# Transposing the softmax maxima of both attentions in bf16 parts, with their copy on ScalarE in both

## The chip, the cores and the metric

The kernel runs as one launch on 1 core of one Trainium2 chip. The metric is the device time of that core in microseconds (us), lower is better. The engines are named as in the profile: PE is TensorE (PEld its weight loads), DVE is VectorE, ACT is ScalarE, POOL is GpSimd, SP is the queue that issues most DMAs.

## What is computed

The input x has 128 sequences of 64 tokens with 128 features, and the context ctx has the same shape. Four blocks follow, each added to x:

```
x = x + attention0(layernorm(x), ctx, ctx, mask)      # 16 heads of 8 features
x = x + ffn0(layernorm(x))                            # 32 experts, top 4
x = x + attention1(layernorm(x), ctx, ctx)            # 16 heads, rotary positions
x = x + ffn1(layernorm(x))                            # 8 experts, top 2

attention:  score = (q @ k.T) / sqrt(8)               # per sequence and head, 64 x 64
            p     = softmax(score, axis=-1)           # subtracts the row's maximum
            out   = (p @ v) @ Wo + bo
```

The change touches the two attentions alone: the way in which each query's maximum reaches the transposed scores from which the exponentials are taken.

## The kernel before, in words

The 8192 tokens are 64 tiles of 128 rows. An attention handles two tiles (four sequences) in one iteration and has 32 iterations; the loop is software-pipelined by hand. Each engine has a `body(i, on)` that works on several iterations at once: `i.at(1)` is the next one, `i.at(-1)` the one before, `i.at(-3)` the third before, and so on. The first four and the last ones are written out; in between a hardware loop holds two iterations. The four blocks of the network follow one another, with the sorting of tokens to experts between them, and experts run after each attention. `attention(layer)` builds both attentions; `layer` 0 takes `body` on DVE and PE, layer 1 `body_with_sums` (DVE) and `body_with_rotation` (PE).

Scores are made twice. `scores(i)` writes the scores of four groups of heads (`UNITS`, r = 0 to 3) with queries on partitions into four PSUM banks `U_[r]`. DVE reduces each bank to its row maxima: `score_unit` (L579), four reductions of 128x512 to 128x8. `turned(i)` then writes the same scores into the same banks with keys on partitions, in which form the exponentials can be multiplied with the values at once. The maximum now belongs to a column, so it has to be subtracted by a matmul:

- `maxima(i)` (L864) turns the maxima `mx` by two fp32 transposes into bank `R_`. It waits for `score_max`, which the fourth reduction raises to its last value.
- In layer 0, `max_rows` on DVE (L586) copies the 128x256 result to `mxT`. In layer 1, ACT does this copy (L810). Either raises `mx_here`.
- `turned(i)` issues the mask matmuls (L873, bf16, layer 0 only), 32 fp32 matmuls of keys by queries (L878), waits for `mx_here`, and issues 16 fp32 matmuls (L890) that subtract the maxima: a constant `max_to` with -1 in the row of the wanted head, times `mxT`. The last four of them raise `t_psum`, on which ACT's exponentials (`exps`, L708) wait.

The order on each engine is the order in which `body` calls its parts. It is written out by hand, and an engine waits at the head of its own list:

- PE, layer 0: scores(i), inputs(next), values(previous), projections(next), rows_turned(i-3) (L972), maxima(i), turned(i), gate(i-3) (L984), output(previous) (L959, L963), next_values(next) (L946). In layer 1 the rotated projections follow turned(i) (L935 and L936 again, by their shared helper), and inputs comes last.
- DVE, layer 0: input statistics (L534, L539), four reductions (L579), the copy (L586), the reciprocal and the division (L619, L621), the gate's logits (L596), the top-k, the output's addition (L643) and its statistics. In layer 1 also the rotary weighting (L627) and the sums of the expert results (L557 to L562).
- ACT, layer 0: the inputs' copy (L788), values (L736), expert rows (L755), the doubled context (L795), the copy of turned rows (L801), keys and queries (L726, L728), `add_normalised` (L768), and then the exponentials (L708), `normalise` (L778).
- POOL, layer 0: among small operations two spreads of keys and queries (L442). Layer 1: eight indirect gathers of expert results per iteration (L419) among small operations.

`hold(engine, semaphore, value)` is a wait followed by an empty instruction, so that the wait is over before the next instruction starts. PE's outputs to `R_` in `maxima` and `output` use the same columns, one after the other.

Of the kernel before, what the change touches and what calls it, by code (L numbers as in the profile page):

```python
# [17 lines left out]
BF16 = mybir.dt.bfloat16  # L18
# [8 lines left out]
P = 128  # L27
# [75 lines left out]
def build(nc, a, out, ts, ys, yt, bias_parts):  # L103

    with ExitStack() as ctx:
        def sb(name, shape, dt=F32):
            return ctx.enter_context(nc.sbuf_tensor(name, shape, dt))
# [37 lines left out]
        sel_of = sb("sel_of", [P, 512], BF16)  # L145
        mx = sb("mx", [P, 2 * P])
        bo3 = [sb(f"bo3_{q}", [P, D], BF16) for q in range(2)]
# [37 lines left out]
        def setup():  # L185
# [39 lines left out]
            def fill(dve):  # L225

                nc.vector.memset(mask_u8.bitcast(F32), 0.0).then_inc(mask_zero, 1)
                nc.vector.memset(power[:], -0.5)
                nc.vector.memset(ones_b[:], 1.0)
                nc.vector.memset(ones_f[:], 1.0)  # L230
                nc.vector.memset(mx[:], 0.0)

            def convert(dve):
# [3 lines left out]
                nc.vector.tensor_copy(seq_of[:], seq_f)  # L237
                nc.vector.tensor_copy(sel_of[:], sel_f)
                nc.vector.tensor_scalar(gate_w[:, 0:E0], gate_w[:, 0:E0], bias_t[:, 8:9], None, ALU.mult)
                dve.wait_ge(mask_in, 16 * 2 * UNITS)  # L240
# [46 lines left out]
            def clear_values(pool):  # L287

                for q in range(2):
# [17 lines left out]
                 "mx_here", "t_psum", "probs", "o_psum", "o_recip", "o_normed", "wo_psum",  # L307
                 "added", "stats_r", "moments_r", "pool_r", "rstd_r", "mean_r", "neg_r", "neg_a", "rows_added", "t_ready", "tt_psum", "tt",
                 "gate_psum", "logits", "top8", "chosen", "top_kept", "row_sum", "combined", "mask_here", "mean_a")
        s = {n: sem(n) for n in names}  # L310

        def attention(layer):
# [10 lines left out]
            Mk = None if layer else carve2(2 * S, BF16)  # L323
            mxT = carve(2 * P)
            Pt = [carve(512) for _ in range(UNITS)]
# [41 lines left out]
            with nc.Block() as block:  # L367
# [162 lines left out]
                def _(dve):  # L530
# [44 lines left out]
                    def score_unit(i, r):  # L575

                        g4 = i.g * UNITS
                        dve.wait_ge(s["score_psum"], g4 + r + 1)
                        nc.vector.tensor_reduce(mx[:].rearrange("p (w c) -> p w c", w=2)[:, :, 32 * r:32 * r + 4],  # L579
                                                U_[r][:, :].rearrange("p (w j k) -> p w j k", w=2, j=4), AX.X, ALU.max  # L580
                                                ).then_inc(s["score_max"], 1)

                    def max_rows(i):

                        dve.wait_ge(s["mx_psum"], i.g + 1)
                        nc.vector.tensor_copy(mxT, R_[:, 0:2 * P]).then_inc(s["mx_here"], 1)  # L586

# [63 lines left out]
                    def body(i, on):  # L651
                        ex, pv, p3 = i.at(2), i.at(-1), i.at(-3)
                        if on(2):
                            hold(dve, x_in[ex.par], (ex.half + 1) * 16)
                            stats(ex, small["st_a"], small["mv_a"], "stats_a", "moments_a")
                        if on(0):
                            for r in range(UNITS):
                                score_unit(i, r)
                            max_rows(i)
                        if on(-1):  # L660
                            divide(pv)
                        if on(-3):
                            read_logits(p3)
                        if on(2):
                            offsets(ex)
                        if on(-3):
                            choose(p3)
                        if on(-1):
                            add_output(pv)
                            output_stats(pv)  # L670

                    def body_with_sums(i, on):
                        nx, pv, p3 = i.at(1), i.at(-1), i.at(-3)
                        if on(0):
                            for r in range(UNITS):
                                score_unit(i, r)
                        if on(-1):
                            divide(pv)
# [26 lines left out]
                def _(act):  # L705
# [78 lines left out]
                    def body(i, on):  # L784
# [21 lines left out]
                        if on(2) and layer:  # L806
                            normalise(ex)
                        if on(0) and layer:
                            act.wait_ge(s["mx_psum"], i.g + 1)
                            nc.scalar.activation(mxT, R_[:, 0:2 * P], ACT.Copy).then_inc(s["mx_here"], 1)  # L810
# [13 lines left out]
                def _(pe):  # L824
# [35 lines left out]
                    def maxima(i):  # L860

                        pe.wait_ge(s["score_max"], (i.g + 1) * UNITS)
                        for w in range(2):
                            last = nc.tensor.transpose(R_[:, w * P:(w + 1) * P], mx[:, w * P:(w + 1) * P], ident[:])  # L864
                        last.then_inc(s["mx_psum"], 1)

                    def turned(i):
# [18 lines left out]
                        for j in range(2):  # L886
                            for r, u in tiles_rb:
# [3 lines left out]
                                    U_[r][64 * u:64 * u + 64, :].rearrange("p (t j q) -> p t j q", t=4, j=2)[:, :, j, :],  # L891
                                    max_to[rows, at:at + S], mxT[rows, :].rearrange("p (t q) -> p t q", t=4),
                                    start=False, stop=True, skip_group_check=True)
# [1070 lines left out]
```

## Time and profile before

| what | value |
|---|---|
| median of 3 runs | 1782.54 us (1778.4 to 1782.55) |
| profiled execution, span | 2270.0 us, mean granted PE clock 0.830 |
| PE busy | 1668.9 us (74%) |
| DVE busy | 1187.1 us (52%) |
| ACT busy | 941.9 us (41%) |
| POOL busy | 1124.3 us (50%) |

The profiled execution is 487 us longer than the median of the runs without a profile; its span is the only time of its own that is shown. In its 40 slices the first attention takes the first 345 us, the second one the stretch from about 1025 to 1666 us; the rest is the sorting and the experts. A line of the profile gives start, length, engine, line, operation and shapes; what stands in square brackets is how long the engine had been idle before it, and what ended that.

### The profile page before, as it was taken

The page shows a single profiled execution, that of the slowest core. Times are in us where ns is not written, and L with a number is a line of the kernel's source. Part 1 is how long each engine was busy: PE and PEld are TensorE (multiplying, and loading weights), DVE is VectorE, ACT ScalarE, POOL GpSimd, SP SyncE. Part 2 cuts the span into 40 slices and gives each one's busy share as a digit, 9 for nine tenths or more (in the row PEclk, how much of TensorE's full clock was granted, in tenths as well). Part 3 has the DMA queues.
Part 4 walks back from the last instruction along what each step waited for, and adds up shares of the span by engine and source line. Part 5 has one row for each costly group of instructions (what it writes and reads, how often), then busy time and mean ns, then how long its engine had stood idle before and what let it go on. Part 6 is the DMA issues. An engine that isn't in the chain of part 4 may idle for free. (4 is left out here: it accounts for less than half of the span.)

```text
span 2270.0 us, 58116 instructions
## 1 busy us (share of the span) xinstructions
PE 1668.9 (74%) x20814; PEld 1246.6 (55%) x20815; DVE 1187.1 (52%) x3485; ACT 941.9 (41%) x2258; POOL 1124.3 (50%) x1456
## 2 busy tenths in 40 slices
PE   6999993947877777826777767777855777777876
PEld 4777771437766677713444444444533555556654
DVE  5778777935555555623455455455666111222245
ACT  3777772723333333413334334344535233333322
POOL 4777761055555565464454454454212555555553
PEclk9999996967787777756888788778875898999888
DMA  4111110012323232521211111111000111111154
GB/s 169 44 42 36 41 30 13 1 44 77 82 77 79 77 85 78 75 59 63 84 41 37 34 40 36 34 39 37 24 14 15 37 40 37 41 40 40 39 143 140
DMA packets 136997, 122.89 MB, mean 54 GB/s; under 512 B 27675, under 2 KB 121915, under 8 KB 136123
## 3 DMA queue, kind: packets, MB, share of 16 engines
q0 software_dynamic: 26624, 56.35, 10.5%
q1 hardware_dynamic: 110078, 64.47, 9.3%
q8 instruction: 68, 1.11, 0.2%
q10 hardware_dynamic: 192, 0.67, 0.1%
q14 instruction: 35, 0.29, 0.0%
HBM read 80.24 MB, written 41.18 MB: 53 GB/s over the span
## 5 line engine op out<-in xcount | busy, mean ns | idle before, releaser
L1488 POOL DMA_INDIRECT arena<-expert_rows,token_of_slot x432 | 413.4, 957 | 402.0 <-issue 221.1
L419 POOL DMA_INDIRECT arena<-slot_results,slot x256 | 246.7, 964 | 118.5 <-issue 86.8
L1879 DVE TENSOR_TENSOR arena<-bank,arena 128x352 f32<-128x352 f32 x144 | 75.5, 524 | 354.3 <-ACT arena L1858 245.4
L1723 POOL DMA_INDIRECT token_results<-arena,slot x144 | 141.1, 980 | 189.9 <-DVE arena L1887 157.0
L909 PE MATMUL bank<-arena,Vp 128*32 128x64 f32 x4096 | 142.8, 230 | 114.6 <-issue 113.1
L1826 PE MATMUL bank<-W,arena 128*128 (+1 forms) x864 | 141.1, 305 | 108.9 <-ACT arena L1865 54.8
L1586 PE MATMUL bank<-arena 128*128 128x128 f32 x1152 | 195.7, 338 | 30.3 <-ACT arena L1633 12.7
L1826 PEld LDWEIGHTS bank<-W,arena 128*128 128x128 f32 (+1 forms) x864 | 127.2, 213 | 164.2 <-issue 156.7
L1812 PE MATMUL bank<-W,arena 128*128 x576 | 214.8, 500 | 1.7 <-ACT arena L1870 1.7
L1586 PEld LDWEIGHTS bank<-arena 128*128 128x128 f32 x1152 | 183.9, 249 | 39.7 <-issue 39.6
L619 DVE RECIPROCAL arena<-bank 128x256 f32<-128x256 f32 x64 | 112.1, 1752 | 173.6 <-PE bank L915 173.6
L909 PEld LDWEIGHTS bank<-arena,Vp 128*32 128x32 f32 x4096 | 90.5, 112 | 168.2 <-issue 166.8
L432 POOL TENSOR_TENSOR arena<-arena,power 128x2 f32<-128x2 f32 x64 | 57.6, 899 | 243.8 <-DVE arena L547 241.0
L579 DVE TENSOR_REDUCE mx<-bank 128x8 f32<-128x512 f32 x256 | 158.3, 680 | 26.7 <-PE bank L853 24.0
L1614 PE MATMUL bank<-W,arena 128*128 x576 | 142.0, 362 | 35.8 <-issue 35.5
L708 ACT ACTIVATE arena<-bank 128x512 f32<-128x512 f32 x256 | 132.2, 603 | 70.4 <-PE bank L890 70.4
L442 POOL TENSOR_TENSOR arena<-arena,fixed 128x1024 f32<-128x1024 f32 x64 | 121.3, 1917 | 50.5 <-ACT arena L726 50.5
L801 ACT ACTIVATE arena<-bank 128x256 f32<-128x256 f32 x64 | 24.5, 383 | 286.0 <-PE bank L972 286.0
L1614 PEld LDWEIGHTS bank<-W,arena 128*128 128x128 f32 x576 | 112.2, 238 | 54.2 <-issue 45.3
L1864 ACT ACTIVATE arena<-bank 128x256 f32<-128x256 f32 x144 | 55.2, 383 | 204.6 <-remote 111.1
L1812 PEld LDWEIGHTS bank<-W,arena 128*128 128x128 f32 x576 | 108.5, 210 | 39.1 <-issue 12.6
L1681 DVE TENSOR_SCALAR arena<-bank,arena 128x128 f32<-128x128 f32 x288 | 99.2, 344 | 51.3 <-remote 34.4
(215 smaller groups left out, 3622.8 us busy)
## 6 DMA issues: line engine op xcount, KB each, us to landing
slot_results<-arena SPq DMA_DIRECT2D x72, 256.0 KB
arena<-in_ctx SPq DMA_DIRECT2D x64, 128.0 KB
expert_rows<-arena SPq DMA_DIRECT2D x64, 128.0 KB
arena<-token_results SPq DMA_DIRECT2D x32, 256.0 KB
arena<-expert_rows,token_of_slot POOLq DMA_INDIRECT x432
W<-in_w SPq DMA_DIRECT2D x4, 1032.0 KB
X<-in_x SPq DMA_DIRECT2D x32, 128.0 KB, 2.1
arena<-slot_results,slot POOLq DMA_INDIRECT x256
```

The lines of the kernel that those rows point to most:

```text
L419: nc.gpsimd.indirect_dma_start(out=gb[i.par][:, to:to + D], out_offset=None, in_=ys, in_offset=bass.IndirectOffsetOnAxis(ap=slot[:, at, k: ...
L442: nc.gpsimd.tensor_tensor(dst[i.par].rearrange("p (b j k) -> p b j k", b=4, j=4), src[i.par].rearrange("p (b k) -> p b k", b=4).unsqueeze( ...
L579: nc.vector.tensor_reduce(mx[:].rearrange("p (w c) -> p w c", w=2)[:, :, 32 * r:32 * r + 4], U_[r][:, :].rearrange("p (w j k) -> p w j k", ...
L619: nc.vector.reciprocal(rec, O_[:, 2 * D:4 * D]).then_inc(s["o_recip"], 1)
L708: nc.scalar.activation(Pt[r], U_[r][:, :], ACT.Exp, scale=SCALE).then_inc(s["probs"], 1)
L909: nc.tensor.matmul(O_[32 * r:32 * r + 32, 64 * sq:64 * sq + 64], Vp[i.par][:, at:at + 32], Pt[r][:, 128 * sq + 64 * j:128 * sq + 64 * j + 64],
L1488: nc.gpsimd.indirect_dma_start(out=XE[n % R][:, c * ROW:(c + 1) * ROW], out_offset=None, in_=ts, in_offset=bass.IndirectOffsetOnAxis(ap=to ...
L1586: last = nc.tensor.matmul(H_[2 * i.par + half][:, at:at + P], Wc[i.par][:, c * W1_0 + u * F0:c * W1_0 + (u + 1) * F0], XT[i.par][:, c * P: ...
L1614: last = nc.tensor.matmul(y, HA[pv.par][:, c * P:(c + 1) * P], W0b[:, bass.ds(x_e, 1), :], start=False, stop=True, skip_group_check=True)
L1723: nc.gpsimd.indirect_dma_start(out=yt[half], out_offset=bass.IndirectOffsetOnAxis(ap=row_of_slot[:, at:at + 1], axis=0), in_=YE[n % 4][:, ...
L1812: last = nc.tensor.matmul(H_[2 * r + u][:, 0:F1], XT[i.par][:, c * P:(c + 1) * P], W1a[:, bass.ds(x_e, 1), u * F1:(u + 1) * F1], start=Tru ...
L1826: last = nc.tensor.matmul(Y_[j.par][:, d * P:(d + 1) * P], AT[d % 2][0:f, k * P:(k + 1) * P], W1b[0:f, bass.ds(x_e, 1), k * P:(k + 1) * P] ...
```

## The change

The maxima are split on DVE into three bf16 parts that add up to the fp32 value (`split_maxima`: a cast, a subtraction, a cast, a subtraction, each waiting for the one before). `mx` becomes compact (128x32), and the parts lie in `mx_parts`, three groups of four columns in each 32. `maxima` turns them by two bf16 matmuls with a bf16 identity, and waits for the fourth step of the split in place of the fourth reduction. `mxT` is bf16, and the constant `max_to` is bf16 with -1 in three rows per head, so the 16 matmuls of `turned` are bf16 and sum the parts. DVE's copy in layer 0 (`max_rows`) goes; ACT makes the copy in both layers, after `add_normalised` and before the exponentials.

```diff
-        mx = sb("mx", [P, 2 * P])
+        mx = sb("mx", [P, 2 * UNITS * 4])
+        mx_parts = sb("mx_parts", [P, 2 * P], BF16)
+        ident_b = sb("ident_b", [P, P], BF16)
+        max_to_b = sb("max_to_b", [P, 4 * S], BF16)
...
                 nc.vector.tensor_copy(sel_of[:], sel_f)
+                nc.vector.tensor_copy(ident_b[:], ident)
+                nc.vector.tensor_copy(max_to_b[:], max_to)
...
-            mxT = carve(2 * P)
+            mxT = carve(2 * P, BF16)
...
-                    def max_rows(i):
-
-                        dve.wait_ge(s["mx_psum"], i.g + 1)
-                        nc.vector.tensor_copy(mxT, R_[:, 0:2 * P]).then_inc(s["mx_here"], 1)
+                    def split_maxima(i):
+
+                        part = [mx_parts[:].rearrange("p (m c) -> p m c", c=32)[:, :, 4 * n:4 * n + 4] for n in range(3)]
+                        rest = mx[:].rearrange("p (m c) -> p m c", c=4)
+                        hold(dve, s["score_max"], (i.g + 1) * UNITS)
+                        nc.vector.tensor_copy(part[0], rest).then_inc(s["max_split"], 1)
+                        hold(dve, s["max_split"], i.g * 4 + 1)
+                        nc.vector.tensor_tensor(rest, rest, part[0], ALU.subtract).then_inc(s["max_split"], 1)
+                        hold(dve, s["max_split"], i.g * 4 + 2)
+                        nc.vector.tensor_copy(part[1], rest).then_inc(s["max_split"], 1)
+                        hold(dve, s["max_split"], i.g * 4 + 3)
+                        nc.vector.tensor_tensor(part[2], rest, part[1], ALU.subtract).then_inc(s["max_split"], 1)
...
                             for r in range(UNITS):
                                 score_unit(i, r)
-                            max_rows(i)
+                            split_maxima(i)
...
                             for r in range(UNITS):
                                 score_unit(i, r)
+                            split_maxima(i)
...
-                        if on(0) and layer:
+                        if on(0):
                             act.wait_ge(s["mx_psum"], i.g + 1)
                             nc.scalar.activation(mxT, R_[:, 0:2 * P], ACT.Copy).then_inc(s["mx_here"], 1)
...
-                        pe.wait_ge(s["score_max"], (i.g + 1) * UNITS)
+                        pe.wait_ge(s["max_split"], (i.g + 1) * 4)
                         for w in range(2):
-                            last = nc.tensor.transpose(R_[:, w * P:(w + 1) * P], mx[:, w * P:(w + 1) * P], ident[:])
+                            last = nc.tensor.matmul(R_[:, w * P:(w + 1) * P], mx_parts[:, w * P:(w + 1) * P], ident_b[:],
+                                                    start=True, stop=True)
...
-                                    max_to[rows, at:at + S], mxT[rows, :].rearrange("p (t q) -> p t q", t=4),
+                                    max_to_b[rows, at:at + S], mxT[rows, :].rearrange("p (t q) -> p t q", t=4),
```

The order of PE's instructions is that of before. On ACT the loop of layer 0 reads so before, from the copy of turned rows to the first exponential:

```order
L801 ACTIVATE arena<-bank 128x256
L726 ACTIVATE arena<-bank,fixed 128x256
L728 ACTIVATE arena<-bank,fixed 128x256
L768 ACTIVATE X<-X,arena 128x128 x2
L707 ISA
L708 ACTIVATE arena<-bank 128x512
```

and so with the change, at the same place (every line number is some 14 higher there):

```order
L815 ACTIVATE arena<-bank 128x256
L740 ACTIVATE arena<-bank,fixed 128x256
L742 ACTIVATE arena<-bank,fixed 128x256
L782 ACTIVATE X<-X,arena 128x128 x2
L824 ACTIVATE arena<-bank 128x256
L721 ISA
L722 ACTIVATE arena<-bank 128x512
```

The new row L824 is the maxima's copy; five instructions stand between the copy of turned rows and it. On DVE, layer 0, the rows from the last reduction to the division read so before:

```order
L579 TENSOR_REDUCE mx<-bank 128x2x4
L585 REGISTER_ALU
L586 COPY arena<-bank 128x256
L619 RECIPROCAL arena<-bank 128x256
L621 TENSOR_TENSOR arena<-bank,arena 128x256
```

and so with the change:

```order
L584 TENSOR_REDUCE mx<-bank 128x2x4
L99 ISA
L593 CAST mx_parts<-mx 128x8x4
L595 TENSOR_TENSOR mx<-mx,mx_parts 128x32
L597 CAST mx_parts<-mx 128x8x4
L599 TENSOR_TENSOR mx_parts<-mx,mx_parts 128x8x4
L632 RECIPROCAL arena<-bank 128x256
L634 TENSOR_TENSOR arena<-bank,arena 128x256
```

The copy is gone, and four small operations stand in its place; in layer 1 the same four are added where no copy stood.

## Rows read from the trace of the kernel before

**Rows 1.** The page: the span, and the group of layer 1's gathers
```profile
span 2270.0 us, 58116 instructions
...
L419 POOL DMA_INDIRECT arena<-slot_results,slot x256 | 246.7, 964 | 118.5 <-issue 86.8
```
**Rows 2.** Windows: stretch, busy us (instructions) by engine, PE clock, DMA share, GB/s
```profile
110.00:120.00 10.00, 9.68 (x262) 7.41 (x269) 7.94 (x26) 7.43 (x18) 7.24 (x13) 1.00 0.14 42
...
1312.00:1316.00 4.00, 2.03 (x21) 0.86 (x19) 0.58 (x1) 0.00 (x0) 3.07 (x5) 0.55 0.19 52
...
1630.00:1641.00 11.00, 9.73 (x247) 7.56 (x247) 9.65 (x32) 7.75 (x18) 2.32 (x8) 1.00 0.01 3
```
**Rows 3.** Timeline of PE, one iteration of layer 0: start, us, engine, line, count, [idle]
```profile
109.41 0.38 PE L972 MATMUL bank<-fixed,arena 128*128 128x128 f32 x2
109.62 0.38 PE L864 MATMUL bank<-fixed,mx 128*128 128x128 f32 x2
109.94 0.42 PE L873 MATMUL bank<-sel_of,arena 32*64 32x512 bf16 x8
110.18 1.14 PE L878 MATMUL bank<-arena 32*64 32x128 f32 x63
...
111.07 1.13 PE L890 MATMUL bank<-arena,fixed 32*64 32x256 f32 x31
112.13 0.63 PE L984 MATMUL bank<-fixed,arena 128*128 128x32 f32 x4
113.08 0.28 PE L959 MATMUL bank<-bo,ones_b 128*128 128x256 bf16 x1 [0.32 <-DVE arena L596]
...
119.30 0.38 PE L972 MATMUL bank<-fixed,arena 128*128 128x128 f32 x2
```
**Rows 4.** Timeline of ACT, the same iteration
```profile
109.83 0.38 ACT L801 ACTIVATE arena<-bank 128x256 f32<-128x256 f32 x1 [0.50 <-PE bank L972]
...
110.82 0.88 ACT L768 ACTIVATE X<-X,arena  x2
112.19 2.06 ACT L708 ACTIVATE arena<-bank 128x512 f32<-128x512 f32 x4 [0.49 <-PE bank L890]
```
**Rows 5.** Timeline of DVE, the same iteration
```profile
110.05 0.42 DVE L586 COPY arena<-bank 128x256 f32<-128x256 f32 x1 [0.83 <-PE bank L864]
...
112.80 0.22 DVE L596 TENSOR_TENSOR arena<-bank,fixed 128x64 f32<-128x64 f32 x1 [0.21 <-PE bank L984]
...
116.27 2.47 DVE L579 TENSOR_REDUCE mx<-bank 128x8 f32<-128x512 f32 x4
...
125.78 0.49 DVE L534 BATCH_NORM_STATS2 arena<-X 128x6 f32 x2 [0.48 <-issue]
```
**Rows 6.** Timelines of layer 1: the copy on ACT, then PE's next matmuls
```profile
1300.70 0.37 ACT L810 ACTIVATE arena<-bank 128x256 f32<-128x256 f32 x1
...
1301.21 1.12 PE L890 MATMUL bank<-arena,fixed 32*64 32x256 f32 x32 [0.24 <-ACT arena L810]
```
**Rows 7.** Timelines of DVE and PE, the first iteration of layer 1 after the gathers
```profile
1626.47 0.25 DVE L539 BATCH_NORM_AGGREGATE arena<-arena 128x2 f32<-128x6 f32 x2
1626.83 0.17 DVE L545 TENSOR_SCALAR arena<-arena 128x2 f32<-128x2 f32 x1
...
1627.06 2.48 DVE L579 TENSOR_REDUCE mx<-bank 128x8 f32<-128x512 f32 x4
...
1629.68 0.41 PE L864 MATMUL bank<-fixed,mx 128*128 128x128 f32 x2 [1.40 <-DVE mx L579]
...
1632.03 0.70 PE L935 MATMUL bank<-arena,Wm 128*128 128x256 f32 x2
...
1633.20 0.88 DVE L627 SCALAR_TENSOR_TENSOR arena<-bank,fixed 128x256 f32<-128x256 f32 x2 [0.76 <-PE bank L936]
```
**Rows 8.** Timelines of POOL and DVE in the setup, where they overlap
```profile
17.50 4.05 POOL L442 TENSOR_TENSOR arena<-arena,fixed 128x1024 f32<-128x1024 f32 x2
...
17.76 2.01 DVE L250 TENSOR_TENSOR arena<-arena 128x256 f32<-128x256 f32 x1
...
21.73 0.43 DVE L254 TENSOR_TENSOR arena<-arena 128x256 bf16<-128x256 f32 x1
```

More of the change, by code:

```diff
@@ L230, in fill @@
                 nc.vector.memset(ones_f[:], 1.0)
-                nc.vector.memset(mx[:], 0.0)
+                nc.vector.memset(mx_parts[:], 0.0)
             def convert(dve):
@@ L307, in build @@
                  "mx_here", "t_psum", "probs", "o_psum", "o_recip", "o_normed", "wo_psum",
-                 "added", "stats_r", "moments_r", "pool_r", "rstd_r", "mean_r", "neg_r", "neg_a", "rows_added", "t_ready", "tt_psum", "tt",
+                 "added", "stats_r", "moments_r", "pool_r", "rstd_r", "mean_r", "neg_r", "neg_a", "rows_added", "max_split", "t_ready", "tt_psum", "tt",
                  "gate_psum", "logits", "top8", "chosen", "top_kept", "row_sum", "combined", "mask_here", "mean_a")
@@ L578, in score_unit @@
                         dve.wait_ge(s["score_psum"], g4 + r + 1)
-                        nc.vector.tensor_reduce(mx[:].rearrange("p (w c) -> p w c", w=2)[:, :, 32 * r:32 * r + 4],
+                        nc.vector.tensor_reduce(mx[:].rearrange("p (w r c) -> p w r c", w=2, r=UNITS)[:, :, r, :],
                                                 U_[r][:, :].rearrange("p (w j k) -> p w j k", w=2, j=4), AX.X, ALU.max
                                                 ).then_inc(s["score_max"], 1)
-                    def max_rows(i):
-                        dve.wait_ge(s["mx_psum"], i.g + 1)
-                        nc.vector.tensor_copy(mxT, R_[:, 0:2 * P]).then_inc(s["mx_here"], 1)
+                    def split_maxima(i):
[9 more added lines that the diff above has]
+                        nc.vector.tensor_tensor(part[2], rest, part[1], ALU.subtract).then_inc(s["max_split"], 1)
                     def read_logits(i):
@@ L1942 @@
              "gate_w": np.concatenate([i["L0_ffn_gate_w"].T, i["L1_ffn_gate_w"].T], axis=1),
-             "max_to": -(np.arange(P)[:, None] % 32 == np.arange(4 * S)[None, :] // S).astype(np.float32),
+             "max_to": -((np.arange(P)[:, None] % 32 < 12)
+                        & (np.arange(P)[:, None] % 4 == np.arange(4 * S)[None, :] // S)).astype(np.float32),
              "den_of": (np.arange(64)[None, :] // 32 * 2 + np.arange(P)[:, None] // S
```

## Prediction

> **What bounds the kernel now.** I first read the page and the table of windows, to see where time goes at all, and then the timelines of PE, ACT and DVE side by side for one iteration of each attention.
>
> The profiled execution is not a good image of the whole. It spans 2270.0 us against a median of 1782.54 [rows 1]. In the second attention PE does 21 matmul records in 4 us, at a granted clock of 0.55, while POOL issues gathers, and waits for nothing that the profile shows [rows 2]. Outside the gathers the same code runs 247 records in 11 us at clock 1.00 [rows 2]. I take the 487 us of excess to be mostly this stall, and the runs without a profile to be without it. So the first attention, which shows no such stall, is read directly, and the second from its iteration after the gathers. All that follows is a difference per iteration, added to 1782.5.
>
> First attention: PE is busy 9.68 of 10 us at clock 1.00 [rows 2], its period is 119.30 - 109.41 = 9.89 us, and in it it waits only 0.32 us, for DVE's logits [rows 3]. PE is the bound. Second attention, after the gathers: PE waits 1.40 us for DVE's reductions before L864, and DVE is busy 9.65 of 11 us [rows 2, 7]. DVE is the bound there, unless POOL is (below).
>
> **The change part by part.** *L890 in bf16.* Its 16 matmuls now take 112.13 - 111.07 = 1.06 us. The nearest rows are the bf16 matmuls of L873: eight with 512 columns in 110.18 - 109.94 = 0.24 us, 30 ns each [rows 3]. Sixteen with 256 columns stream the same number of columns, so 0.24 us is the lower bound. But L878 issues 32 matmuls (two records each) in 0.89 us, 28 ns each [rows 3], so I find no matmul faster than 28 ns, whatever its columns: upper end 16 x 30 ns = 0.48. I take 16 x 28 ns, rounded down, 0.43: the cost of an instruction, not of its columns. Saved: 0.63 us. The Trainium skill (TensorE: Matmul & The Clock Gate, "Back-to-back issue gap") gives small matmuls a floor of about 25 ns each; an estimate by it is 0.40 us. These rows agree.
>
> *L864 in bf16.* From 0.32 us [rows 3] to between 0.1 and 0.32; I take 0.2.
>
> *Copy in layer 0, DVE to ACT.* On DVE the copy ran at 110.05 and ended 0.6 us before PE wanted it [rows 3, 5]. On ACT it is queued behind L801, L726, L728 and `add_normalised` (L768), and L801 can't start before PE has turned the rows (L972). From L972: 0.42 to L801, 0.99 to L768, 0.88 for L768's two less 0.07 of overlap, 0.37 for the copy and 0.14 until PE goes on (1301.21 less 1301.07) [rows 3, 4, 6]: 2.73 us from L972 to L890. Before it was 111.07 - 109.41 = 1.66. So PE waits for ACT, and L890 starts 1.07 us later behind L972. The new closed path is 2.73 + 0.43 + the unchanged 119.30 - 112.13 = 7.17 from L984 to the next L972: **10.33 us against 9.89, +0.44**. With L890 at 0.24 or 0.48 it is +0.25 or +0.49. The exponentials take 2.06 us and start after L890 as before [rows 4]; the matmuls behind them move with them.
>
> *Four split steps.* Each is a small DVE operation behind a `hold`. The nearest rows are L539 and L545: 0.11 us between the end of one and the start of the dependent next, and 0.17 for the small one [rows 7]. Four times 0.28 are 1.12 us. Bounds: 0.7 (no gap) and 1.6. In layer 0 this path, counted from L890, is 0.43 + 0.67 to the logits L596 + 3.47 to the reductions + 2.47 + 1.12 + 0.14 to the transposes [rows 3, 5, 7], 8.30 us; then 0.2 + 0.24 + 0.89 for L864, L873 and L878 = 9.63 before L890 can follow. Every second iteration has DVE 0.36 later (the 0.48 idle at the loop's head [rows 5]): 9.99. Both are under 10.33, so ACT's queue hides the split, with 0.34 to 0.70 us to spare. DVE itself has room: it loses the copy's 0.34 and 0.83 of waiting [rows 5].
>
> 29 of the 32 iterations have `add_normalised`: 29 x 0.44 = **+12.8 us**.
>
> *Layer 1, L864 to the rotation.* From the reductions' end (1629.54) PE needed 0.14 to L864, 2.35 more to L935, and 1.17 more until DVE could weigh the rotated part (1633.20), 3.66 us, of which DVE idled 0.76 [rows 7]. Now: 1.12 + 0.14 + (2.35 - 0.63 - 0.12) + 1.17 = 4.03, and DVE's own list 2.90 + 1.12 = 4.02. Either way +0.36. The copy is no obstacle: ACT reaches it while DVE still splits. 27 iterations with expert sums: +9.7 us if DVE paces them. But POOL may pace them: eight gathers are 8 x 0.96 = 7.7 us busy, and with their idle time (246.7 + 118.5) / 256 x 8 = 11.4 [rows 1]; with a guess of 3 us of small operations that brackets the 12.7 us of DVE's period. If POOL paces, the change costs nothing there. Bounds 0 and 9.7; I take the middle, **+5**.
>
> *Setup and ends.* Two more casts, about 0.5 us, and the first iteration's split, which PE waits for; the last iterations of layer 1, where DVE is ahead, gain a little. **+1**.
>
> Sum: 12.8 + 5 + 1 = 18.8, 1782.5 + 18.8 = **1801 us**. Against the profiled execution's own 2270.0 the sum differs, since there PE is the bound in the stalled iterations: 27 x (0.63 + 0.12) = -20, so 2270 + 14 - 20, about 2264.
>
> **The rivals.** *A measured run is stalled like the profile.* Then layer 1 is paced by PE and gains 20 us where I add 5: 1782.5 + 12.8 - 20 + 1 = 1776, **faster**. For it speaks that the stall is in every iteration with gathers; against it, that 487 us have to go somewhere when no profile is taken. It decides if more than a third of those iterations stall.
>
> *ACT is not late.* If L801 starts with less delay or the operations before the copy overlap more, layer 0 follows DVE's path, (9.63 + 9.99) / 2 = 9.81, -0.08 an iteration, -2 us; with layer 1 at 0 to 9.7 that is 1781 to 1791. For it speaks that 1.07 us of lateness rests on one row each; against it, that ACT's idle 0.50 before L801 names L972 as what it waits for.
>
> *A collision of split and spread.* In the setup a DVE operation on two SBUF operands took 2.01 us while POOL ran L442, and 0.43 when it did not [rows 8]. In layer 0, L442 would start some 0.3 us after the split ends. If a split step falls under it, it is 1.6 us later, the path is 9.81 + 1.6 = 11.4, +1.5 an iteration, +44: about 1833. The Trainium skill (GPSIMD Engine Reference, "Key points") says that the two engines contend where DVE has two SBUF inputs; rows 8 agree. It decides once the split is late by 0.3 us.
>
> **How the numbers follow.** My forecast has 0.63: slower, own range 1790 to 1812 (layer 0 at +0.25 and layer 1 at 0; layer 0 at +0.49, layer 1 at 9.7 with a split of 1.3 us). The stalled rival has 0.18, ACT not late 0.12 (half of it within 0.3%), the collision 0.07. Taking in all but the collision and the far edge of the first, the range is 1774 to 1816. About 0.3%, 5.3 us, is what a measurement can tell: faster 0.18, same 0.09, slower 0.73.
>
> **What would show it.** In the new profile, layer 0: PE's matmuls of maxima (bf16, x16) in 0.43 us, just before them idle time of 0.3 us or more ended by ACT's copy, the period at 10.3, PE busy less than 9.4 of 10 us. Idle before the transposes ended by DVE's split. In layer 1 after the gathers: the wait for the split 1.1 us longer than that for the reductions, and no idle of DVE before L627. The forecast is wrong if layer 0's period stays under 9.9, or if the split takes under 0.8 us.

## The result, and the profile after

The changed kernel takes **1824.49 us** (median of 4 runs, 1821.58 to 1828.69) against 1782.55 us for the one before: a ratio of 1.0235 [1.0214, 1.0257], some 42 us slower. I had forecast 1801 us, slower, in a range of 1774 to 1816. The direction is right, and the time lies outside the range.

The page of the changed kernel, its span, the busy times and the granted clock in 40 slices:

```profile
span 1823.2 us, 56618 instructions
PE 1384.7 (76%) x19790; PEld 1076.7 (59%) x19791; DVE 1220.5 (67%) x3711; ACT 962.5 (53%) x2290; POOL 1127.2 (62%) x1456
...
PEclk9999999969899999999588988888895699999988
```

The profiled run itself took 1825.04 us, so this profile stands for the runs. The profile of before did not [rows 1]: the same kernel, profiled again (experiment e0 below), spans 1779.2 us. Everything of layer 1 is therefore compared with e0. Its page:

```profile
span 1779.2 us, 58116 instructions
...
PEclk9999999959899999998579999999985799999987
```

The two spans differ by 44.0 us. To place them I follow the first and the last transposes of the maxima (L864 before, L878 now; 32 iterations) on PE:

| stretch | before (e0) | after | difference |
|---|---|---|---|
| layer 0, first transposes at | 28.52 | 32.85 | +4.3 |
| layer 0, first to last transposes | 307.84 | 318.39 | +10.6 |
| layer 1, first to last transposes | 403.91 | 432.76 | +28.9 |

These three are 43.8 us of the 44.0, so nothing else moved. Two thirds of the loss is in layer 1, where I had placed 5 us.

**Layer 0, steady state.** Timeline of PE after, two iterations (start, us, engine, line, operation, count, [idle before, and what ended it]):

```profile
125.68 0.38 PE L987 MATMUL bank<-fixed,arena 128*128 128x128 f32 x2
126.20 0.29 PE L878 MATMUL bank<-ident_b,mx_parts 128*128 128x128 bf16 x2
128.39 0.42 PE L905 MATMUL bank<-arena,max_to_b 32*64 32x256 bf16 x16 [0.57 <-ACT arena L824]
128.74 0.63 PE L999 MATMUL bank<-fixed,arena 128*128 128x32 f32 x4
...
135.91 0.38 PE L987 MATMUL bank<-fixed,arena 128*128 128x128 f32 x2
136.92 0.28 PE L878 MATMUL bank<-ident_b,mx_parts 128*128 128x128 bf16 x2 [0.63 <-DVE mx_parts L599]
138.62 0.42 PE L905 MATMUL bank<-arena,max_to_b 32*64 32x256 bf16 x16
```

From one L987 to the next it is 10.23 us where it was 9.89 [rows 3]. In the first iteration the maxima's matmuls L905 wait 0.57 us for ACT's copy L824. In the second PE waits 0.63 us for the split before L878, but L905 still starts 2.71 us behind L987, as in the first, and again 0.15 us behind the end of the copy, so the copy sets both. ACT's list in the first iteration, with the copy (L824) behind `add_normalised` (L782):

```profile
126.10 0.38 ACT L815 ACTIVATE arena<-bank 128x256 f32<-128x256 f32 x1 [0.50 <-PE bank L987]
...
127.09 0.88 ACT L782 ACTIVATE X<-X,arena  x2
127.86 0.38 ACT L824 ACTIVATE arena<-bank 128x256 bf16<-128x256 f32 x1
128.85 1.57 ACT L722 ACTIVATE arena<-bank 128x512 f32<-128x512 f32 x3 [0.61 <-PE bank L905]
```

The copy ends at 128.24 and L905 starts 0.15 us later. DVE's split in the same iteration, behind the last reduction:

```profile
122.53 2.45 DVE L584 TENSOR_REDUCE mx<-bank 128x8 f32<-128x512 f32 x4
125.08 0.18 DVE L593 CAST mx_parts<-mx 128x32 bf16<-128x32 f32 x1
125.37 0.19 DVE L595 TENSOR_TENSOR mx<-mx,mx_parts 128x32 f32<-128x32 f32 x1
125.66 0.18 DVE L597 CAST mx_parts<-mx 128x32 bf16<-128x32 f32 x1
125.95 0.19 DVE L599 TENSOR_TENSOR mx_parts<-mx,mx_parts 128x32 bf16<-128x32 f32 x1
```

The reductions end at 124.98, the split at 126.14: 1.16 us, four steps 0.28 to 0.29 us apart.

**Layer 0, first iteration.** DVE's first two split steps, the POOL spread that runs beside them, and PE waiting for the fourth step:

```profile
29.46 0.87 DVE L593 CAST mx_parts<-mx 128x32 bf16<-128x32 f32 x1
30.44 1.77 DVE L595 TENSOR_TENSOR mx<-mx,mx_parts 128x32 f32<-128x32 f32 x1
```

```profile
28.38 3.78 POOL L447 TENSOR_TENSOR arena<-arena,fixed 128x1024 f32<-128x1024 f32 x2
```

```profile
32.85 0.39 PE L878 MATMUL bank<-ident_b,mx_parts 128*128 128x128 bf16 x2 [5.78 <-DVE mx_parts L599]
```

The same place in e0, where PE waits for the reductions alone:

```profile
28.52 0.69 PE L864 MATMUL bank<-fixed,mx 128*128 128x128 f32 x2 [3.29 <-DVE mx L579]
```

The cast took 0.87 us and the subtraction 1.77 us, where they take 0.18 and 0.19 in steady state. The third and fourth steps, behind the spread's end at 32.16, took 0.18 and 0.19 here too, and e1, e3, e4 and e10 show the same four durations within 0.01 us. Against e0, PE is 4.3 us late, and this is never made up.

**Layer 1.** PE before (e0), two iterations in the middle of the loop:

```profile
1102.73 0.44 PE L864 MATMUL bank<-fixed,mx 128*128 128x128 f32 x2 [1.20 <-DVE mx L579]
...
1105.36 0.70 PE L935 MATMUL bank<-arena,Wm 128*128 128x256 f32 x2
...
1115.94 0.44 PE L864 MATMUL bank<-fixed,mx 128*128 128x128 f32 x2 [1.20 <-DVE mx L579]
```

and after, with L936 and L950 of before as L951 and L965:

```profile
1102.65 0.29 PE L878 MATMUL bank<-ident_b,mx_parts 128*128 128x128 bf16 x2 [1.61 <-DVE mx_parts L599]
...
1104.36 0.70 PE L950 MATMUL bank<-arena,Wm 128*128 128x256 f32 x2
1104.89 0.59 PE L951 MATMUL bank<-arena,Wm 128*128 128x256 f32 x2
1105.76 1.09 PE L965 MATMUL bank<-Wm,arena 128*64 128x128 f32 x16
...
1116.22 0.28 PE L878 MATMUL bank<-ident_b,mx_parts 128*128 128x128 bf16 x2 [2.61 <-DVE mx_parts L599]
...
1118.42 1.22 PE L950 MATMUL bank<-arena,Wm 128*128 128x256 f32 x2
1119.44 1.06 PE L951 MATMUL bank<-arena,Wm 128*128 128x256 f32 x2
1120.83 1.09 PE L965 MATMUL bank<-Wm,arena 128*64 128x128 f32 x16
```

Before, PE waits 1.20 us for the reductions, and the rotated projections (L935, L950 after) take 0.70. After, the wait for the split is up to 2.65 us in the middle of the loop, and behind the second such wait here the same matmuls take 1.22. Windows of the changed kernel over these matmuls in the two iterations (stretch, length, busy us of PE, PEld, DVE, ACT, POOL with instructions, PE clock, DMA share, GB/s):

```profile
1104.30:1105.50 1.20, 1.20 (x11) 1.04 (x7) 1.20 (x3) 0.95 (x2) 1.11 (x2) 1.00 0.14 41
1118.40:1120.40 2.00, 2.00 (x10) 1.62 (x6) 0.68 (x2) 1.96 (x4) 1.36 (x3) 0.50 0.13 33
```

The first ran at 1.00 and the second at 0.50, the two levels of 2.4 and 1.2 GHz. From L878 to L965 it is 3.11 us in the first iteration and 4.61 in the second: 1.5 us lost. In 31 iterations after, 23 waits before L878 are longer than 2 us, and L950 is slow (over 0.8 us) behind 15 of them; of the 8 shorter waits 2 are followed by a slow L950. In e0 it is slow in 2 of 31. Windows of the middle of layer 1, in the same columns, before (e0):

```profile
1020.00:1300.00 280.00, 231.04 (x5405) 177.10 (x5393) 235.58 (x723) 189.79 (x449) 197.03 (x278) 0.99 0.20 54
```

and after:

```profile
1020.00:1300.00 280.00, 220.01 (x4626) 170.96 (x4610) 235.30 (x756) 176.90 (x418) 203.89 (x278) 0.89 0.20 56
```

POOL and DVE are about as busy as before, and one gather takes 970 ns on average where it took 972 in e0, so the gathers did not become slower. PE has the lower clock, 0.89 for 0.99, and fewer instructions done.

### The profile page after: what moved, and what is told of

It reads as the page before. It is cut to its first block and busy times, and to the rows that moved or that the text cites. A ratio compares the mean times of both kernels' runs of the same rounds, so it can differ in the third digit from the quotient of the medians.

```text
span 1823.2 us, 56618 instructions
## 1 busy us (share of the span) xinstructions
PE 1384.7 (76%) x19790; PEld 1076.7 (59%) x19791; DVE 1220.5 (67%) x3711; ACT 962.5 (53%) x2290; POOL 1127.2 (62%) x1456
## 3 DMA queue, kind: packets, MB, share of 16 engines
q8 instruction: 65, 1.06, 0.2%
## 5 line engine op out<-in xcount | busy, mean ns | idle before, releaser
L1827 PE MATMUL bank<-W,arena 128*128 x576 | 199.5, 471 | 0.9 <-ACT arena L1885 0.9
L1601 PE MATMUL bank<-arena 128*128 128x128 f32 x1152 | 146.6, 283 | 0.0
L1601 PEld LDWEIGHTS bank<-arena 128*128 128x128 f32 x1152 | 139.3, 198 | 0.3
L1546 PE MATMUL bank<-fixed,arena 128*128 128x128 f32 x288 | 48.1, 291 | 109.4 <-DMA arena<-expert_rows,token_of_slot 109.4
L730 ACT ACTIVATE arena<-arena,fixed 128x256 f32<-128x256 f32 x256 | 105.7, 495 | 33.3 <-DVE arena L651 33.3
L1827 PEld LDWEIGHTS bank<-W,arena 128*128 128x128 f32 x576 | 100.9, 195 | 33.6 <-issue 4.3
L1873 ACT ACTIVATE arena<-bank 128x352 f32<-128x352 f32 x144 | 66.7, 463 | 95.6 <-PE bank L1827 95.6
L1431 PE MATMUL bank<-arena 128*128 128x288 f16 (+1 forms) x384 | 86.1, 394 | 39.7 <-DVE arena L1372 21.2
L1657 ACT ACTIVATE arena<-bank,fixed 128x512 f32<-128x512 f32 x72 | 49.4, 687 | 115.3 <-PE bank L1546 115.0
L1629 PE MATMUL bank<-W,arena 128*128 x576 | 105.6, 306 | 0.0
L1879 ACT ACTIVATE arena<-bank 128x256 f32<-128x256 f32 x144 | 55.2, 383 | 94.5 <-PE bank L1852 94.5
```

The source lines that it names most:

```text
L730: last = nc.scalar.activation(dst[i.par].rearrange("p (b j k) -> p b j k", b=4, j=4)[:, :, j, :], src[i.par].rearrange("p (b k) -> p b k", ...
L1601: last = nc.tensor.matmul(H_[2 * i.par + half][:, at:at + P], Wc[i.par][:, c * W1_0 + u * F0:c * W1_0 + (u + 1) * F0], XT[i.par][:, c * P: ...
L1629: last = nc.tensor.matmul(y, HA[pv.par][:, c * P:(c + 1) * P], W0b[:, bass.ds(x_e, 1), :], start=False, stop=True, skip_group_check=True)
L1827: last = nc.tensor.matmul(H_[2 * r + u][:, 0:F1], XT[i.par][:, c * P:(c + 1) * P], W1a[:, bass.ds(x_e, 1), u * F1:(u + 1) * F1], start=Tru ...
```

## The experiments

The theory after the result: layer 0 loses to ACT's late copy, and layer 1 loses because the longer wait lets PE's granted clock fall. The main rivals: the split itself lengthens layer 1's path by 1 us an iteration, clock or no clock; or POOL and its gathers are slower for some reason that has nothing to do with PE. All medians below come with the ratio to the kernel before, on the same chip; span figures are of each kernel's own profile.

| kernel | median us | ratio to before [95%] | layer 0, first to last | layer 1, first to last | PE clock, 1020 to 1300 us |
|---|---|---|---|---|---|
| e0, before again | 1781.13 | one run | 307.84 | 403.91 | 0.99 |
| after | 1824.49 | 1.0235 [1.0214, 1.0257] | 318.39 | 432.76 | 0.89 |
| e1, change in layer 0 alone | 1795.40 | 1.0073 [1.0056, 1.0090] | 318.68 | 404.75 | 0.99 |
| e2, change in layer 1 alone | 1810.87 | 1.0159 [1.0142, 1.0176] | 309.10 | 432.06 | 0.90 |
| e3, after, PE kept busy | 1800.54 | 1.0110 [1.0093, 1.0127] | 316.33 | 411.66 | 1.00 |
| e4, after, copy first on ACT | 1806.52 | 1.0141 [1.0114, 1.0168] | 303.98 | 432.48 | 0.88 |
| e5, rounded maxima, no split | 1769.54 | 0.9928 [0.9911, 0.9944] | 295.45 | 404.93 | 0.93 |
| e6, e5 with PE kept busy | 1769.48 | 0.9922 [0.9903, 0.9942] | 296.61 | 405.71 | 0.96 |
| e7, before, PE kept busy | 1782.08 | 0.9994 [0.9984, 1.0003] | 308.55 | 405.53 | 1.00 |
| e8, before, copy on ACT | 1810.34 | 1.0160 [1.0143, 1.0176] | 337.92 | 405.80 | 0.99 |
| e9, before, split in layer 1 | 1837.78 | 1.0313 [1.0296, 1.0330] | 307.41 | 461.98 | 0.91 |
| e10, e3 and e4 together | 1785.10 | 1.0026 [1.0015, 1.0038] | 303.96 | 409.98 | 1.00 |
| e11, e5 with DVE's copy | 1766.44 | 0.9916 [0.9899, 0.9932] | 296.30 | 405.28 | 0.94 |

**e0: the kernel before, profiled once more.** No edit.

> The kernel before, unchanged, for a second profile. If the stall of its first profile (span 2270 us) belongs to that one execution, this one spans about 1781 us, and the second attention's period shows what paced it: theory A (DVE alone) expects 12.7 us; theory B (PE's clock already halves in some iterations, because PE waits for DVE's reductions) expects 13.0 to 13.3 with some rotation matmuls at 1.22 us instead of 0.70. If the stall is the kernel's own, the span is again above 2200.

Measured: one time of 1781.13 us, span 1779.2, clock 0.99 through the gathers where the first profile had a stretch of 0.55 [rows 2]. The 487 us were one execution's. What stalled it stays open: between 1100 and 1500 us of that profile PE stood still for 77.9 us inside the row of its value matmuls (L909), with nothing that the profile shows to wait for. Layer 1's middle iterations take 13.10 us on average, not the 12.7 that I had read behind the gathers, and DVE idles up to 1.06 us for the rotated projections in each.

**e1 and e2: the change in one layer alone.** In the other layer the reductions write fp32 columns, PE transposes them in fp32, and the copy is where it was before. The core of e1 (the comment is added here):

```diff
-            mxT = carve(2 * P, BF16)
+            mxT = carve(2 * P) if layer else carve(2 * P, BF16)
...
-                            split_maxima(i)      # layer 1
...
-                        pe.wait_ge(s["max_split"], (i.g + 1) * 4)
+                        if layer:
+                            pe.wait_ge(s["score_max"], (i.g + 1) * UNITS)
+                        else:
+                            pe.wait_ge(s["max_split"], (i.g + 1) * 4)
```

> The change in the first attention alone; the second as before. By the two traces the first attention costs about 15 us (11 in its loop, 4 at its start), so the sum of the parts gives 1797 us. If the loss sits in the first attention, this stays near 1824; if it all sits in the second, 1783.

> The change in the second attention alone; the first as before (its copy on VectorE too). By the sum of the parts 1782.5 + 27 = 1810 us. My prediction had 1782 to 1792 for it. If the parts do not add up (one attention's ends hide the other's loss), the two single changes together differ from 42 us by more than 5.

Measured: 1795.40 and 1810.87 us, both as expected. Against 1782.55 they are +12.9 and +28.3, together 41.2 of the 42: the two layers' losses add up, and the larger is layer 1's.

**e3: the changed kernel with PE kept busy ahead of its long wait.** In layer 1 PE issues 24 bf16 matmuls of 128 columns into unused columns of bank `R_`, before it waits for the split:

```diff
+                        if layer:
+                            for _ in range(24):
+                                nc.tensor.matmul(R_[:, 3 * P:4 * P], ident_b[:], ones_b[:], start=True, stop=True)
                         pe.wait_ge(s["max_split"], (i.g + 1) * 4)
```

> The changed kernel, with 24 extra bf16 matmuls of 128 columns into unused PSUM columns before TensorE waits for the split in the second attention. Clock theory: the rotation matmuls stay at 0.70 us, the period falls from 14.15 us towards 13.1 to 13.4, total 1798 to 1808. Rival (VectorE's own list or GpSimd's gathers pace it, the clock is a symptom): no gain, 1822 to 1830. Rival 2 (extra matmuls only delay): slower than 1830.

Measured: 1800.54 us, as expected. PE in an iteration of layer 1, the added matmuls (L879), the transposes (L882) and the rotated projections (L954):

```profile
1104.72 1.50 PE L879 MATMUL bank<-ones_b,ident_b 128*128 128x128 bf16 x24
1107.48 0.28 PE L882 MATMUL bank<-ident_b,mx_parts 128*128 128x128 bf16 x2 [1.26 <-DVE mx_parts L600]
...
1109.05 0.70 PE L954 MATMUL bank<-arena,Wm 128*128 128x256 f32 x2
```

and its window, in the columns above:

```profile
1020.00:1300.00 280.00, 231.71 (x5397) 187.06 (x5397) 248.64 (x799) 186.80 (x441) 205.27 (x282) 1.00 0.21 57
```

The added matmuls take 1.50 us of PE's time and do nothing, the split is in place, and the wait behind it is no longer than before the change. The projections are back at 0.70 in 29 of 31 iterations, and layer 1 is 21.1 us shorter. Nothing but PE's activity changed, so these 21 us of the 28.9 were the clock. (The median fell by 24; of that 2.1 us are in layer 0, which this edit does not touch.) What is left is 411.66 - 403.91 = 7.8 us, inside the 0 to 9.7 that I had given the split. In this window DVE no longer waits for the rotated projections, where it waited 21.9 us in all in e0: DVE's own list paces layer 1 now, as forecast. POOL is close behind: in the same window it waits for DVE only 5.0 us in all.

**e7: the control.** The kernel before with 8 such matmuls in layer 1.

```diff
+                        if layer:
+                            for _ in range(8):
+                                nc.tensor.matmul(R_[:, 3 * P:4 * P], seq_of[:], ones_b[:], start=True, stop=True)
                         pe.wait_ge(s["score_max"], (i.g + 1) * UNITS)
```

> Control: the kernel before with 8 extra bf16 matmuls ahead of the same wait in the second attention. Its granted clock there is already 0.99, so the clock theory expects no gain beyond 5 us: 1777 to 1784. If extra matmuls help for another reason, this one gains 15 us or more.

Measured: 1782.08 us, ratio 0.9994. Where the clock is already at 0.99, keeping PE busy gains nothing. So e3 did not uncover a gain that was always to be had.

**e4: ACT's copy ahead of `add_normalised` in layer 0.**

```diff
+                        if on(0) and not layer:
+                            act.wait_ge(s["mx_psum"], i.g + 1)
+                            nc.scalar.activation(mxT, R_[:, 0:2 * P], ACT.Copy).then_inc(s["mx_here"], 1)
                         if on(-3) and not layer:
                             add_normalised(old)
```

> The changed kernel with ScalarE's copy of the maxima ahead of add_normalised in the first attention. Theory (ScalarE's queue delays the copy in one iteration of two, VectorE's split delays the transposes in the other): the 0.57 us of waiting for the copy goes, both iterations fall to VectorE's path of about 9.6 and 9.95, the average from 10.23 to 9.8, -10 to -13 us: 1811 to 1815. If the split alone sets both, nothing changes (1824).

Measured: 1806.52 us, 18 us faster than the changed kernel and more than I expected. PE in layer 0, the transposes (L881) and the maxima's matmuls (L908):

```profile
123.33 0.29 PE L881 MATMUL bank<-ident_b,mx_parts 128*128 128x128 bf16 x2
...
124.76 0.42 PE L908 MATMUL bank<-arena,max_to_b 32*64 32x256 bf16 x16
...
133.29 0.29 PE L881 MATMUL bank<-ident_b,mx_parts 128*128 128x128 bf16 x2 [0.63 <-DVE mx_parts L599]
...
142.75 0.29 PE L881 MATMUL bank<-ident_b,mx_parts 128*128 128x128 bf16 x2
```

L908 waits no more, and periods of 9.96 and 9.46 us alternate, 9.71 on average, each second one set by the split. That is 0.18 us better than the kernel before and 0.52 better than after, and 31 of these are 16 us (14.4 from the first to the last transposes, by the table, and nearer 17 by the two ratios). Layer 1 has its 432 us as before the edit: this repair does not touch the clock.

**e8: the copy on ACT alone.** The kernel before, with `max_rows` taken off DVE in layer 0 and ACT's copy in both layers; fp32 throughout, no split.

```diff
-                            max_rows(i)
...
-                        if on(0) and layer:
+                        if on(0):
                             act.wait_ge(s["mx_psum"], i.g + 1)
```

> The kernel before with one thing of the change: ScalarE makes the copy of the maxima in the first attention too, behind add_normalised. By the rows, TensorE goes on with L890 2.73 us after L972 in place of 1.66, with nothing gained back: +1.07 a period in 29 iterations, +31 us, 1813. If the copy's place did not matter, 1782.

Measured: 1810.34 us, as expected. The maxima's matmuls (L889) on PE in layer 0:

```profile
118.64 1.12 PE L889 MATMUL bank<-arena,fixed 32*64 32x256 f32 x32 [0.78 <-ACT arena L809]
...
129.57 1.12 PE L889 MATMUL bank<-arena,fixed 32*64 32x256 f32 x32 [0.78 <-ACT arena L809]
```

The period is 10.93 us, 1.04 above before. The copy's move alone costs 28 us (30 in the loop of layer 0, by the table), and in the change the bf16 matmuls give back 0.70 us of it in each iteration.

**e10: both repairs together** (the edits of e3 and e4).

> The changed kernel with both repairs: the copy ahead of add_normalised in the first attention, and 24 extra bf16 matmuls in the second. If the two losses are separate, the gains add: 1824.5 - 18 - 24 = 1782.5, within 4 us of the kernel before.

Measured: 1785.10 us, as expected; 18.0 + 24.0 = 42.0 us were gained one by one, and 39.4 together. The loops alone add up more closely: 14.4 us in layer 0 (e4) and 21.1 in layer 1 (e3) one by one, 14.4 and 22.8 together. With its copy in a good place and its clock held, the exact split is 1.0026 [1.0015, 1.0038] of the kernel before: what the bf16 matmuls save in the loop of layer 0 (3.9 us against e0) the split takes back in layer 1 (6.1) and in the first iteration (4.0).

**e9: the split without the bf16 matmuls, in layer 1.** Layer 0 as before. In layer 1 PE waits for the four split steps, but transposes and subtracts the fp32 maxima by the old matmuls; the split works on a constant of zeros beside them, so its result is not used.

```diff
-                        pe.wait_ge(s["score_max"], (i.g + 1) * UNITS)      # layer 1
+                        pe.wait_ge(s["max_split"], (i.n + 1) * 4)
                         for w in range(2):
-                            last = nc.tensor.transpose(R_[:, w * P:(w + 1) * P], mx[:, w * P:(w + 1) * P], ident[:])
+                            last = nc.tensor.transpose(R_[:, w * P:(w + 1) * P], mx_wide[:, w * P:(w + 1) * P], ident[:])
```

> The first attention as before; in the second VectorE does the four split steps on a constant and TensorE waits for them, but transposes and subtracts the maxima in fp32 as before. So TensorE's wait is longer by 1.15 us, but its list is 0.8 us longer than with the change, and its wait is therefore about 2.0 to 2.3 us instead of 2.3 to 2.6. If the clock falls with the length of this wait, fewer iterations fall than in e2: total between 1795 and 1811. If only the split's time counts, about 1791 with the clock at 0.99; if the bf16 matmuls themselves lower the clock, also 1791 or so.

Measured: 1837.78 us, a miss, slower than the whole change. PE in layer 1, the transposes (L891) and the rotated projections (L965) of two iterations:

```profile
1106.22 0.44 PE L891 MATMUL bank<-fixed,mx_wide 128*128 128x128 f32 x2 [2.66 <-DVE mx_parts L608]
...
1108.74 0.70 PE L965 MATMUL bank<-arena,Wm 128*128 128x256 f32 x2
...
1120.61 0.44 PE L891 MATMUL bank<-fixed,mx_wide 128*128 128x128 f32 x2 [2.61 <-DVE mx_parts L608]
...
1124.25 1.05 PE L965 MATMUL bank<-arena,Wm 128*128 128x256 f32 x2
```

From the first of these transposes to the second it is 14.39 us, at full clock: undisturbed iterations at full clock take 14.24 to 14.41, some 1.2 more than the 13.10 of e0. From the reductions' end to the split's end it is 1.26 and 1.33 us in turn. In the middle of the loop those with a slow L965 (13 of 31 in all, behind waits of the same 2.6 us) take 15.7 to 17.07. I had expected the split to be paid in part out of slack; there is none. Reductions, split, transposes, turned scores, rotated projections and the weighting on DVE are one closed path, on which DVE waits for PE (0.83 to 1.06 us before its weighting) and PE for DVE in the same iteration. So a split of 1.3 us costs 1.2, and shorter matmuls on this path give theirs back (0.75 by the forecast, which left 0.36 net; e3's middle iterations take 13.36, 0.26 more than e0's). The clock comes on top: 462 - 404 = 58 us are, as an estimate, 28 x 1.2 = 34 for the split and 24 for the clock; counted one by one, the 14 disturbed iterations in the middle of the loop take 26 us more than 14.3 us each would. It follows too that the shortened list is not what makes the wait long in the change: with the old fp32 matmuls it is 2.6 us as well, since a longer list also makes the next reductions later. A lower clock costs the fp32 list more: from the transposes to the rotated projections the slowest iterations take 4.27 us where undisturbed ones take 2.5, and in the changed kernel 2.70 where they take 1.6.

**e5: maxima rounded by the reductions themselves.** The exponentials need the same shift for all keys of a query, not the exact maximum. The reductions write bf16 straight into the first part, the split goes, the other two parts stay zero, and the copy stands as in e4. What is subtracted is thus the maximum rounded to bf16.

```diff
-                        nc.vector.tensor_reduce(mx[:].rearrange("p (w r c) -> p w r c", w=2, r=UNITS)[:, :, r, :],
+                        nc.vector.tensor_reduce(mx_parts[:].rearrange("p (w c) -> p w c", w=2)[:, :, 32 * r:32 * r + 4],
...
-                            split_maxima(i)
...
-                        pe.wait_ge(s["max_split"], (i.g + 1) * 4)
+                        pe.wait_ge(s["score_max"], (i.g + 1) * UNITS)
```

> No split: the reductions write the maxima straight as bf16 (one part, rounded), with the copy ahead of add_normalised in the first attention and everything else as changed. Subtracting a rounded maximum leaves the softmax as it is, since the same number is taken off the row's sum. First attention: TensorE's list of 9.15 us, 9.2 to 9.4 a period, 15 to 20 us under the kernel before. Second: VectorE's list as before, 13.1 us a period if the clock holds; TensorE waits about 1.9 us for the reductions, and if that lets the clock fall as the split did, it loses 5 to 15. Total 1762 to 1782.

Measured: 1769.54 us, 0.9928 [0.9911, 0.9944] of the kernel before: faster than both by the interval, though by under 1%. Layer 0's period is 9.47 us. Layer 1 is 404.93, no shorter than before; waits of up to 2.83 us before the transposes remain in it, and the clock still falls behind some of them (0.93 in the table).

**e6: e5 with 12 added matmuls in layer 1.**

> As e5, with 12 extra bf16 matmuls before TensorE waits for the reductions in the second attention. If the clock falls there in e5, this one is 5 to 15 us faster than e5; if not, equal to it. 1758 to 1768 in either case.

Measured: 1769.48 us, no gain. The clock rose from 0.93 to 0.96 and layer 1 kept its 405 us. DVE's sums of the expert results show why:

```profile
1112.83 0.69 DVE L563 TENSOR_TENSOR arena<-arena 128x512 f32<-128x512 f32 x1 [1.30 <-DMA arena<-slot_results,slot]
1126.06 0.69 DVE L563 TENSOR_TENSOR arena<-arena 128x512 f32<-128x512 f32 x1 [1.34 <-DMA arena<-slot_results,slot]
```

They wait 1.3 us for a gather to land. These two are 13.23 us apart, and the next gap is 13.58; e5 has the same waits, 10 of them between 1020 and 1300 us. So in the middle of the loop the gathers pace layer 1 in both, and what the clock costs there is hidden. This is the bound by POOL's gathers that the prediction left open. It lies at 13.2 to 13.6 us, just above the 13.10 of the kernel before. e6 settles less than e3, since its 12 matmuls left the clock at 0.96.

**e11: e5 with the copy on DVE in layer 0**, as before the change.

> As e5 (bf16 maxima straight from the reductions), with VectorE's copy in the first attention in place of ScalarE's. TensorE should no longer wait 0.42 us for the copy; the first attention's period falls from 9.47 to between 9.1 and 9.3: 1759 to 1766. If VectorE's list becomes the bound there, 1769 or more.

Measured: 1766.44 us, 0.9916 [0.9899, 0.9932], the lowest median of all, just above the 1759 to 1766 that I expected; its interval overlaps that of e5, so the two are not told apart. It too subtracts the rounded maximum. The maxima's matmuls (L909) and the output's first matmul (L978) in layer 0:

```profile
118.89 0.48 PE L909 MATMUL bank<-arena,max_to_b 32*64 32x256 bf16 x15
...
120.59 0.28 PE L978 MATMUL bank<-bo,ones_b 128*128 128x256 bf16 x1 [0.67 <-DVE arena L614]
```

The period of L909 is 9.48 us. PE now waits 0.67 us for the gate's logits on DVE, where it waited 0.32 before [rows 3]: part of what the bf16 matmuls save is lost there.

## Why the prediction was right and wrong

- **The profile of before is a stalled execution.** Right, and shown by e0. The rival that measured runs stall too falls with it: all runs of before, on every chip, are within 1778.4 and 1786.34 us.
- **Layer 0 is bound by PE at 9.89 us.** Right: e0 has the same 9.89.
- **L890 in bf16, 0.43 us.** Somewhat too high: 128.74 - 128.39 = 0.35 us for 16, 22 ns each. My floor of 28 ns for any matmul, "the cost of an instruction, not of its columns", was a misreading of an average. By their starts in the trace the 16 matmuls go in two groups of eight, most of them 3 to 4 ns apart inside a group and the second group 108 ns behind the first; the fp32 records of L878, from which the 28 ns came, begin in the same way. That changes 0.43 to 0.35 and not the mechanism of the delay.
- **The copy on ACT is late: 2.73 us from L972 to L890, period 10.33, +12.8 us.** Right in mechanism and nearly in size: 2.71 us, period 10.23, +10.6. (The overlap ahead of the copy was 0.11, not 0.07.) With 0.35 in place of 0.43 the sum gives 10.25. e8 isolates the move (10.93 against 10.96 by the same sum with fp32 matmuls), and e4 undoes it. The rival "ACT is not late" is what e4 made; its period of 9.71 stands against the 9.81 worked out for it.
- **The split takes 1.12 us and is hidden in layer 0.** Right: 1.16 us from the reductions' end, and covered by ACT's 10.23.
- **Collision of split and spread.** Wrong as a steady state (no period near 11.4), but real in the first iteration. The term "setup and ends, +1" was 4.3 at its start, where the spread stretched the first two steps by 2.3 us together; the price of 1.6 for one step was right (1.58 for the subtraction).
- **Layer 1: +0.36 us an iteration if DVE paces, 0 if POOL does, taken as +5.** This is the step that failed. The path's own growth was sized right: e3 leaves 7.8 us. But the sum took PE's durations at full clock from [rows 7] for granted. The change lengthens PE's wait in layer 1 from 1.20 to as much as 2.65 us, by the split ahead of it (in e9 it is as long with the old matmuls). Behind such waits the clock falls to its lower level in about half of the iterations, at 1.5 us each where it does. Seventeen slow iterations at 1.5 are 25 us; e3 recovers 21 in layer 1 and 24 in all. No rival had this, although [rows 2] showed the clock at 1.00 and at 0.55.
- **The base of 12.7 us in layer 1** was too low as well; it is 13.1 with gathers. That error did not enter the sum.

By terms: layer 0 +10.6 (forecast 12.8), ends +4.3 (1), layer 1's path +7.8 (5), the clock +21 (none). What stays open is what else decides whether the clock falls behind a wait: in the changed kernel it did so behind 15 of 23 waits over 2 us and not behind the other 8, and e9 has both with waits of equal length (2.6 us).

## What to carry to other kernels

When a change makes later what PE waits for, work out PE's new idle time and ask at which clock the matmuls behind it will run: a row of a few matmuls behind a long wait, compared with its twin behind a short one, shows it. Before moving a small copy to an engine with room on average, count what stands ahead of it in that engine's list from the moment its input is there; here its place cost 14 us of the loop (e4), and 28 with the fp32 matmuls (e8), and the engine's busy share said nothing. And ask whether the number needs to be exact: a softmax shift rounded once, written by the reduction itself, needed no split, and with it the bf16 matmuls paid.

## What the runs showed of the hardware that I had not expected

- Sixteen bf16 matmuls of 32 x 256 went in 0.35 us, and not at a fixed price each: they started in two groups of eight, most of them 3 to 4 ns apart inside a group, with 108 ns from one group's start to the next.
- Behind waits of over 2 us PE ran at its lower clock in 15 of 23 cases in the changed kernel and in 13 of 25 in e9, by the first row of rotated projections behind each. Matmuls that compute nothing, 1.50 us in each iteration, brought back 21 us of layer 1 (e3), while the same in a kernel whose clock held brought none (e7).
- Two small DVE operations on SBUF data took 0.87 and 1.77 us beside a POOL spread, and 0.18 and 0.19 without it. The subtraction, on 32 columns, grew by 1.58 us, as much as the one on 256 columns in the setup [rows 8]; the cast grew by 0.69.
- One profiled execution was 487 us longer than every other run of the same kernel.
